# Gated cross-attention with routed experts: row-sum reciprocals moved from DVE to POOL, and the weighted sum one step further behind the scores

## The reference

```python
# x [8, 512, 256], ctx [8, 1601, 256], 16 heads of 16 columns
def xattn(q, kv):
    qh, kh, vh = heads(q @ Wq.T), heads(kv @ Wk.T), heads(kv @ Wv.T)
    attn = einsum('bhnc,bhlc->bhnl', qh * D ** -0.5, kh)
    attn = softmax(attn, axis=2)                  # over the queries n, not over l
    attn = attn / sum(attn, axis=-1, keepdims=True)   # then each query's row over l
    return merge(einsum('bhnl,bhlc->bhnc', attn, vh)) @ Wo.T
x = x + tanh(g_xattn) * xattn(layernorm(x), ctx)
x = x + tanh(g_ffn) * top2_of_8_experts(layernorm(x))
```

## Time and profile before

| what | value |
|---|---|
| time, median of 3 runs | 1932.16 us (1930.76 to 1936.4) |
| the profiled execution's own time | 1939.25 us |
| its span, first to last instruction | 1937.5 us |
| mean granted TensorE clock, share of full speed | 0.968 |
| busy: PE, DVE, ACT, POOL | 1677.6, 1404.7, 1290.5, 559.3 us |
| busy share: PE, DVE, ACT, POOL | 87%, 73%, 67%, 29% |

### The profile page before, as it was taken

One profiled execution on the slowest core, in us unless ns is written; L12 is line 12 of the kernel. 1 busy time (PEld: TensorE's weight loads), 2 busy tenths in 40 slices (PEclk: granted clock), 3 DMA queues, 4 the chain that ended last, 5 costly groups with the idle time before them and its releaser, 6 DMA issues. The chain is left out here.

```text
span 1937.5 us, 35084 instructions
## 1 busy us (share of the span) xinstructions
PE 1677.6 (87%) x9776; PEld 889.2 (46%) x9888; DVE 1404.7 (73%) x2269; ACT 1290.5 (67%) x3634; POOL 559.3 (29%) x837
## 2 busy tenths in 40 slices
PE   5549889989978989998898998887289999999997
PEld 3213223323313323332332332211189999999997
DVE  1448999989889998898999989998344444444443
ACT  2459989999998998998999899998011111111111
POOL 5123125135125223413513522212312222222222
PEclk9879999999999999999999999999599999999999
DMA  5954942961891594396288168312712222222222
GB/s 138 172 89 83 138 82 64 124 128 47 127 150 59 91 145 84 75 120 122 65 118 147 50 101 109 71 44 72 290 33 35 35 38 35 35 38 35 36 38 27
DMA packets 124986, 169.16 MB, mean 87 GB/s; under 512 B 14321, under 2 KB 102257, under 8 KB 124817
## 3 DMA queue, kind: packets, MB, share of 16 engines
q1 hardware_dynamic: 102064, 136.77, 40.6%
q0 software_dynamic: 13344, 17.90, 5.6%
q10 hardware_dynamic: 9408, 12.58, 1.8%
HBM read 117.96 MB, written 49.24 MB: 86 GB/s over the span
## 5 line engine op out<-in xcount | busy, mean ns | idle before, releaser
L660 ACT ACTIVATE w_all<-scores,negmax 128x512 f32<-128x512 f32 (+1 forms) x1664 | 1120.7, 717 | 65.5 <-DVE negmax L811 48.7
L811 DVE TENSOR_REDUCE negmax<-scores 128x2 f32<-128x1024 f32 (+1 forms) x832 | 1000.3, 1215 | 125.3 <-PE scores L550 120.1
L550 PE MATMUL scores<-q_stack,w_all 128*128 128x512 bf16 (+1 forms) x1552 | 480.6, 387 | 159.2 <-ACT w_all L660 141.0
L563 PE MATMUL acc<-w_all,vz 128*32 128x512 f32 (+1 forms) x3328 | 447.3, 610 | 10.9 <-POOL vz L935 9.4
L550 PEld LDWEIGHTS scores<-q_stack,w_all 128*128 128x128 bf16 (+1 forms) x1664 | 113.5, 100 | 636.3 <-ACT w_all L660 493.8
L660 ACT ACTIVATION_READ_ACCUMULATOR w_all<-scores,negmax 128x1 f32 (+1 forms) x1664 | 393.0, 236 | 0.0
L1129 ACT ACTIVATE hidden<-ps_hidden 128x512 f32<-128x512 f32 x142 | 84.9, 598 | 429.1 <-PE ps_hidden L1092 429.1
L935 POOL TENSOR_TENSOR vz<-w_all,rz 128x68 f32<-128x68 f32 (+1 forms) x416 | 125.2, 301 | 850.3 <-DVE rz L797 833.2
L1092 PEld LDWEIGHTS ps_hidden<-rows_t,w_sb 128*128 128x128 f32 x2272 | 266.4, 193 | 5.7 <-DVE rows_t L1156 1.7
L1092 PE MATMUL ps_hidden<-rows_t,w_sb 128*128 128x128 f32 x2272 | 267.3, 276 | 1.1 <-DVE rows_t L1156 1.0
L1105 PE MATMUL ps_y<-w_sb,hidden 128*128 128x256 f32 x1136 | 256.8, 379 | 0.0
(11 more groups left out here) (134 smaller groups left out, 1005.7 us busy)
## 6 DMA issues: line engine op xcount, KB each, us to landing
w_all<-k_parts SPq DMA_DIRECT2D x256, 200.1 KB, 8.1
q_stack<-q_parts SPq DMA_DIRECT2D x256, 64.0 KB, 7.6
w_all<-in_ctx_t SPq DMA_DIRECT2D x8, 1601.0 KB
k_parts<-parts SPq DMA_DIRECT2D x42, 300.0 KB, 2.9
w_all<-in_w ACTq DMA_DIRECT2D x12, 1024.0 KB, 11.7
rows<-routed SPq DMA_DIRECT2D x71, 129.0 KB, 2.1
q_parts<-parts SPq DMA_DIRECT2D x14, 384.0 KB, 7.2
k_parts<-parts SPq DMA_DIRECT2D x14, 300.8 KB, 3.3
```

The source lines that it names most:

```text
L550: mm = pe.matmul(scores[0:r, 2 * (u % SLOTS) + j % 2, :], k_stack[:, g, j, lt * P:lt * P + r], q_stack[:, g, j, :], start=True, stop=True)
L563: mm = pe.matmul(acc[32 * j:32 * j + 32, :], vz[0:r, s % RING, j, :], probs[0:r, s % RING, j, :], start=(lt == 0), stop=(lt == LT - 1))
L660: e = act.activation(probs[0:r, s % RING, j, :], scores[0:r, 2 * (u % SLOTS) + j % 2, :], ACT.Exp, bias=negmax[0:r, u % 4, j % 2:j % 2 + 1 ...
L811: dve.tensor_reduce(negmax[0:r, u % 4, :], scores[0:r, 2 * (u % SLOTS):2 * (u % SLOTS) + 2, :], AX.X, ALU.max, negate=True).then_inc(negma ...
```

## The change

The reciprocal leaves DVE. `weigh_values` on POOL now waits for the exponentials itself, forms `rz` as `z` to the power -1 with a tensor of -1.0 (`minus_one`, set once on DVE), waits for its own result, and scales the values. `weigh` on PE stands at the end of step s+3 instead of s+2, through the new constant `LAG`; `take_acc` on DVE moves with it by one step. So that `acc` of the last group is copied out before it is turned, fill `o_turn 3` moves from step 3 to step 4, and fill `k 1` from step 4 to step 3. The rings keep their four places.

```diff
+LAG = 3
...
-    2: ("next", "k", 0), 3: ("tail", "o_turn", 3), 4: ("next", "k", 1), 5: ("tail", "attn_turn", 1),
+    2: ("next", "k", 0), 3: ("next", "k", 1), 4: ("tail", "o_turn", 3), 5: ("tail", "attn_turn", 1),
...
+        minus_one = sb("minus_one", [P, GH])
...
-                    if s >= 2 and it.cur:
-                        weigh(it.b, s - 2)
-                    if s < 2 and it.tail:
-                        weigh(it.b - 1, STEPS + s - 2)
+                    if s >= LAG and it.cur:
+                        weigh(it.b, s - LAG)
+                    if s < LAG and it.tail:
+                        weigh(it.b - 1, STEPS + s - LAG)
...
-            def reciprocals(b, s):
-
-                r = rows_of(s % LT)
-                dve.wait_ge(exp_done, b * UNITS + 2 * s + 2)
-                dve.reciprocal(rz[0:r, s % RING, :], z[0:r, s % RING, :]).then_inc(rz_ready, 1)
-
...
-                        if p == 1 and s == 1 and it.tail:
+                        if p == 1 and s == LAG - 1 and it.tail:
                             take_acc(b - 1, G - 1)
-                        if p == 1 and it.cur and s in (LT + 1, 2 * LT + 1, 3 * LT + 1):
+                        if p == 1 and it.cur and s in (LT + LAG - 1, 2 * LT + LAG - 1, 3 * LT + LAG - 1):
                             take_acc(b, s // LT - 1)
-                        if p == 1 and s == 0 and it.tail:
-                            reciprocals(b - 1, STEPS - 1)
-                        if p == 1 and s > 0 and it.cur:
-                            reciprocals(b, s - 1)
...
+                pool.wait_ge(exp_done, b * UNITS + 2 * s + 2)
+                pool.tensor_tensor(rz[0:r, s % RING, :], z[0:r, s % RING, :], minus_one[0:r, :], ALU.pow).then_inc(rz_ready, 1)
                 pool.wait_ge(rz_ready, b * STEPS + s + 1)
```

More of the change, by code:

```diff
@@ L333, in attention_and_routing @@
         ROUTE_STEPS, PLACE_STEPS = 25, 6
-        DVE_SETUP = 6 + 2 * E
+        DVE_SETUP = 7 + 2 * E
         def load_w1(eng, e):
@@ L670, in _ @@
         def _(dve):
-            for tile, value in ((v_ones[:, :, :, :, DH], 1.0), (vz[:, :, :, :], 0.0), (minus_half[:, :], -0.5),
+            for tile, value in ((v_ones[:, :, :, :, DH], 1.0), (vz[:, :, :, :], 0.0), (minus_half[:, :], -0.5), (minus_one[:, :], -1.0),
                                 (zero[:, :], 0.0), (seen[:, :], 0.0), (ones_e[:, :], 1.0)):
```

## The result

The changed kernel takes 1970.83 us (median of 4 runs, 1968.62 to 1987.82), the kernel before 1932.43 us on the same chip: a ratio of 1.0202 (95% interval 1.0165 to 1.0238), 38 us more. The profiled execution took 1970.26 us, 31.0 more than that of before. The loss is in the attention: the last exponential ends at 1379.1 us where it ended at 1348.9, and what follows it takes 589.4 us where it took 588.6.

What follows compares the result with a forecast made beforehand. ACT, DVE and PE, all nearly full, hand units round a short ring; none sets the pace everywhere. Terms -3 + 11 + 3 + 1 = +12 us on the median 1932.16 gave 1944 us, own range 1936 to 1956, reaching to 1923 and 1960.

Steps and rivals of the forecast that it cites:

- the first mechanism: POOL's queue in steps 12 to 17 makes scaled values 1.8 us late for PE in step 19: +11 us.
- steps 44 to 51: With a DMA each step, POOL needs 2.83 us against 2.68, falls 1.2 us behind within the lag: nothing.
- The queue of steps 12 to 17: Powers, layer norms and k fills meet on POOL; PE waits 1.8 us in batches 1 to 6: +11 us.
- ACT waits of the same size: PE's waits of 1 to 2 us around step 19 pass on to ACT at equal length.
- The power's price: On POOL, each power takes about 1.04 us, 1.17 us a step with its wait.
- the lag takes it all: Rival: the longer lag hides POOL's lateness in steps 12 to 17, no change, 1933 us; chance 0.27.
- The relief of DVE: Reciprocals leaving DVE save 0.07 us in each of a few steps per batch: -3 us, bounds -29 and 0.
- DVE was the brake: Rival: DVE sets the pace of half the steps and POOL keeps up, so faster, 1912 us; chance 0.16.
- The moved copy and fills: `take_acc` one step later and neighbouring k fills, in steps 2 to 4 and 41: +3 us, bounds 0 and 11.
- The end chain: After batch 7's last exponential, a power replaces a reciprocal with nothing covering the chain: +1 us.
- The rival with two bounds: Rival: at 1.5 us a power, POOL is late in steps 12 to 17 and 44 to 51, 1966 us; chance 0.09.
- Its own range: The forecast's range for the whole kernel, with the bounds of the queue and the moved copy: 1936 to 1956 us.

Runs made afterwards that it cites:

- e6_hybrid_both: Changed kernel with the reciprocals of steps 10 to 17 and 43 to 51 back on DVE, 35 powers left on POOL; ratio to the kernel before 1.0004.
- e5_hybrid_mid: Changed kernel with the reciprocals of steps 10 to 17 back on DVE, 44 powers left on POOL; ratio to the kernel before 1.0062.
- e13_pool_unrolled: Changed kernel with POOL's batches 1 to 5 written out in place of its hardware loop; ratio to the kernel before 1.0081.
- its control: Kernel before the change with POOL's hardware loop written out, nothing else changed; ratio to the kernel before 0.9958.
- e3_cheap: Changed kernel with the power replaced by a multiplication by -1, so the reciprocal is left out; ratio to the kernel before 0.9981.
- e1_lag_only: Changed kernel with all reciprocals back on DVE, keeping the lag of three steps and the moved fills; ratio to the kernel before 1.0002.
- e8_all: Changed kernel with reciprocals of steps 10 to 17 and 43 to 51 on DVE and fill k 0 in step 1; ratio 0.9936, repeated 0.9971.
- e16_only51: Changed kernel with the reciprocals of steps 10 to 17 and 43 to 50 on DVE, step 51's power kept on POOL; ratio to the kernel before 0.9999.

## Why the prediction was wrong

The direction and the first mechanism held, the size did not: +12 forecast, +38 measured, outside the range of 1923 to 1960 us.

- **The step that failed** is the sentence on steps 44 to 51: "Over eight steps POOL falls 1.2 us behind, less than the step of lag: nothing." A step needs 3.00 us of POOL, not 2.83, against 2.65 of the others, so POOL falls 8 x 0.35 = 2.8 us behind; and the sum ended with the batch, while POOL then turns its loop. That turn stood in the trace of before, in the 3.8 to 4.6 us for which POOL idles at the start of batches 2 to 5; the trace puts one of them down to DVE's reciprocals and three to PE (`POOL vz L935 <- PE acc L563: 14.9, 4, 4.6`, a row that the prediction did not read), and the turn was hidden. Measured: 0.6% (`e6_hybrid_both` against `e5_hybrid_mid`) to 0.8% (`e13_pool_unrolled` less its control), 11 to 15 us in place of 0; by the steps it is (2.92 - 1.3) x 6 = 10 us, some of it the clock of the worst step 2.
- **The queue of steps 12 to 17** (+11, bounds 0 and 16) was the right mechanism at the right place. PE waited 1.94 us in step 19, 1.8 was said; with the smaller waits before it the queue costs 2.3 us a batch, 14 us.
- **What a wait of PE sets off** was taken as "ACT waits of the same size". This failed too: in four of six batches the granted clock fell to half behind the wait, 10 us that no term held. Queue and clock together are 24 us by the steps and 27 by `e5_hybrid_mid`.
- **The power's price** was right: 1013 ns, and 1.19 us to what depends on it (642.93 to 644.12), against 1.17. Of the rivals, "the lag takes it all" needed 0.87 us or less; `e3_cheap` shows that with 0.20 us it does.
- **The relief of DVE** (-3): `e3_cheap` less `e1_lag_only` is -0.2%, 4 us, which agrees in size, but the intervals overlap, so it can't be told from nothing. "DVE was the brake" needed POOL to keep up and then 1912 us; in `e3_cheap` POOL keeps up, and 0.9981 is 1929.
- **The moved copy and fills** (+3) cost 1.3 us in step 2 of each of six batches, 8 in all, but with the longer lag and what other steps win back they sum to nothing (`e1_lag_only`, 1.0002). The end chain (+1) took 0.8 us more, and the experts stayed.
- **The rival with two bounds** (1966, chance 0.09) named both places. Its reason, a dearer power, was wrong; its chance was set by that reason alone, and no other way to the same lateness was asked for.
- **Its own range**, 1936 to 1956, is not what its bounds add up to: with the queue and the copy at theirs the sum runs from 1930 to 1957 us. The measured time lies above either.

## What to carry to other kernels

Follow a lagging engine's queue past the end of the stretch, into whatever comes next on that engine: a loop's turn that is hidden while the engine waits becomes visible once the engine is late. Count a wait of PE at more than its length, since the clock may fall behind it (in four of six batches here), and look for the batches in which the same step takes twice as long. And move work to the slow engine only in the steps where it has room: 35 of 52 powers cost nothing that could be told, all 52 cost 2%.

## What was not expected of the hardware

- TensorE, at full clock (2.4 GHz) in the stretch ahead, was granted 0.50 to 0.61 of it on average in the rows above, its lower level of 1.2 GHz for most of them, right behind waits of 1.94 and 2.98 us and while it was then busy nearly all the time. Behind the like wait of step 19 it fell in four batches of six (in batches 1, 3 and 5 well into step 20). With PE given work in that wait it stayed at 1.00 in all six.
- The turn of the hardware loop (compare-and-branch to next instruction) takes about 0.3 us or ten times that and more, and which of the two goes by the kernel and engine, alike at all four turns of a run. On POOL it takes 3.4 to 4.5 us in the kernel before, 5.0 to 7.2 in the changed one and 0.3 in `e6_hybrid_both`, `e8_all` and `e16_only51`; on DVE 3.0 to 3.9 us before and 0.3 to 0.4 after. The Trainium skill (Runtime: NRT & Kernel Launch, section "Instruction fetch mechanics") says that a taken branch whose target is outside the instructions held at the engine has to fetch them by DMA before it goes on. The two levels, and the two instruction transfers in the turn of 5.5 us, agree with that; which part of the code was held, no run here shows.
- The same POOL instructions cost more inside the hardware loop than written out: a step of power, scaling and DMA issue 3.00 against 2.67 us.
